# Products with the values: two quads of heads one behind the other, and scores by single heads

## What is computed

```python
q, k, v = _split_heads(query, W_Q), _split_heads(key, W_K), _split_heads(value, W_V)
scores = jnp.einsum('bhqd,bhkd->bhqk', q, k) / np.sqrt(D_K)
scores = jnp.where(mask[:, None, :, :] == 1, -1e9, scores)
p = jax.nn.softmax(scores, axis=-1)
ctx = jnp.einsum('bhqk,bhkd->bhqd', p, v)
out = jnp.einsum('bsd,ed->bse', concat(ctx), W_O) + residual
mu, var = mean(out), mean((out - mu) ** 2)
return (out - mu) * rsqrt(var + LN_EPS) * gamma + beta
```

## Time and profile before

| | us |
|---|---|
| median of 3 runs | 192.54 (192.52 to 193.17) |
| the profiled execution | 192.26 |
| its span, first to last instruction | 190.4 |
| TensorE busy | 160.2 (84%) |
| VectorE busy | 138.4 (73%) |
| GpSimd busy | 104.9 (55%) |
| ScalarE busy | 100.7 (53%) |
| block 0 (starts at 28.02) | 26.0 |
| block 1 (starts at 54.02) | 20.1 |
| blocks 2, 3 and 4 | 18.3 each |
| blocks 5 and 6 | 15.3 and 13.7 |

### The profile page before, as it was taken

How to read it: one execution, slowest core, us unless ns; L and a number is a source line. 1 busy time by engine, 2 the same in 40 slices (tenths; PEclk the granted TensorE clock), 3 DMA queues, 4 the chain that set the end, 5 groups by cost and what they waited for, 6 DMA issues and landing times.

```text
span 190.4 us, 3486 instructions
## 1 busy us (share of the span) xinstructions
PE 160.2 (84%) x1208; PEld 86.2 (45%) x1208; DVE 138.4 (73%) x300; ACT 100.7 (53%) x133; POOL 104.9 (55%) x128
## 2 busy tenths in 40 slices
PE   7697939798869999999999999999899898977300
PEld 7454515343324466445544554564455363534200
DVE  1775533875856669788978897798989965685993
ACT  3242144634544664666755875587577679473400
POOL 6002441434544371349597959664744946858990
PEclk9999996999988999999999999999999999999955
DMA  5959988746989985873596664747350051020115
GB/s 174 358 152 159 284 210 237 220 121 114 275 218 229 232 205 149 246 233 102 161 280 176 186 195 131 204 129 218 135 201 0 3 179 46 6 104 0 54 56 220
DMA packets 23083, 31.42 MB, mean 165 GB/s; under 512 B 3459, under 2 KB 18611, under 8 KB 23067
## 3 DMA queue, kind: packets, MB, share of 16 engines
q1 hardware_dynamic: 22234, 29.98, 55.4%
q10 hardware_dynamic: 832, 1.23, 2.0%
HBM read 11.28 MB, written 4.19 MB: 81 GB/s over the span
## 4 chain that ended last, share of the span: by engine, by line
PE 61%; DVE 13%; DMA 12%; ACT 4%; issue 4%; POOL 2%; SPq 1%; DVEq 1%; POOLq 0%; ACTq 0%
PE pv_ps L818 14%; PE work_ps L828 13%; PE work_ps L761 11%; PE scores_ps L809 11%; PE max_ps L782 8%; DVE neg_max L599 4%; DMA R<-neg_max_t 4%; DMA x_t<-in_x_cols 3%; DMA R<-first_max_t 3%; DMA R<-q 2%; DVE ctx_q L607 2%; ACT probs L496 2%; POOL y L366 1%; ACT not_full L450 1%; DVE var_eps_last L723 1%
## 5 line engine op out<-in xcount | busy, mean ns | idle before, releaser
L496 ACT ACTIVATE probs<-scores_ps 77x1024 f32<-77x1024 f32 x64 | 64.6, 1017 | 47.6 <-PE scores_ps L809 42.3
L599 DVE TENSOR_REDUCE neg_max<-max_ps 128x6 f16<-128x462 f32 (+1 forms) x84 | 45.6, 566 | 13.9 <-PE max_ps L782 13.8
L809 PE MATMUL scores_ps<-R,kb 126*77 126x512 f16 x128 | 39.7, 394 | 3.7 <-DMA R<-first_max_t 1.9
L782 PEld LDWEIGHTS max_ps<-kb,R 125*128 125x128 f16 x512 | 27.1, 100 | 34.3 <-DVE neg_max L599 16.9
L339 POOL TENSOR_TENSOR q<-q 128x512 f16<-128x512 f32 x14 | 16.2, 1155 | 43.6 <-ACT q L457 43.6
L818 PE MATMUL pv_ps<-probs,v_all 77*32 77x512 f32 x256 | 34.3, 608 | 4.2 <-ACT probs L496 3.5
L782 PE MATMUL max_ps<-kb,R 125*128 125x77 f16 x512 | 32.8, 202 | 3.4 <-DVE neg_max L599 2.5
L346 POOL TENSOR_TENSOR ctx_n<-ctx_q,rden 128x256 f32<-128x256 f32 x32 | 20.1, 628 | 21.9 <-DVE rden L609 21.8
L607 DVE STREAM_TRANSPOSE ctx_q<-pv_ps 128x512 f32<-128x512 f32 x32 | 22.8, 711 | 10.1 <-PE pv_ps L818 9.7
L828 PE MATMUL work_ps<-wo_t,ctx_e 128*128 128x256 f32 x112 | 26.9, 382 | 0.0
L761 PE MATMUL work_ps<-x_t,wq_t 128*128 128x512 f32 x48 | 24.6, 635 | 0.4
(11 more groups left out here) (70 smaller groups left out, 143.6 us busy)
## 6 DMA issues: line engine op xcount, KB each, us to landing
R<-mask_t SPq DMA_DIRECT2D x14, 616.0 KB
R<-q SPq DMA_DIRECT2D x48, 128.0 KB
x_t<-in_x_cols SPq DMA_DIRECT2D x8, 512.0 KB, 6.7
y<-in_x SPq DMA_DIRECT2D x8, 512.0 KB, 4.7
out<-y SPq DMA_DIRECT2D x7, 512.0 KB, 2.6
mask_i<-in_mask_cols SPq DMA_DIRECT2D x8, 154.0 KB
out<-y SPq DMA_DIRECT2D x2, 256.0 KB, 2.9
kb<-k SPq DMA_DIRECT2D x12, 38.5 KB, 3.3
```

Of the source, the lines that this page charges most:

```text
L496: nc.scalar.activation(probs[:, s, :, :], scores_ps[s % 2][0:KEYS, :, :], ACT.Exp).then_inc(exp_done, 1)
L599: nc.vector.tensor_reduce(to[:, t, lo:hi], max_ps[u % 2][:, 0:(hi - lo) * KEYS].rearrange("p (h k) -> p h k", k=KEYS), AX.X, ALU.max, nega ...
L782: last = nc.tensor.matmul(max_ps[u % 2][:, (h - lo) * KEYS:(h - lo + 1) * KEYS], R[m % R_RING][0:MAX_ROW, h, t * P:(t + 1) * P], kb[0:MAX_ ...
L809: last = nc.tensor.matmul(scores_ps[s % 2][0:KEYS, i, :], kb[:, 2 * s + i, n // PER_BATCH, :], R[n % R_RING][:, 2 * s + i, :], start=True, ...
```

## The change

The eight banks are dealt out anew: three banks for scores, each of one head, two for the maximum units as before, two for quads (`pv_both`) and one for the rest. Each head's scores now have their own semaphore step, and the product of a head waits for the exponential of the head three before. ScalarE's exponential is one instruction for each head, 77x512.

The quads move. Step 4 of block n does quads 0 and 1, and step 0 of block n + 1 quads 2 and 3. In the last block quad 2 stands in step 6, and quad 3 after the last step, as before. VectorE's turns follow in the same steps, its turning back of the second half goes from step 1 to step 2, and GpSimd's divisions move accordingly. The wait for the scaled queries of block 1 stands ahead of block 0 and not in it, since their projection now uses a bank of scores and one of quads.

The diff, cut to its core:

```diff
@@ -60,6 +60,11 @@
 Y_RING = 4
 R_RING = 3
 
+SCORES_RING = 3
+MAX_RING = 2
+
+PV_RING = 2
+
 
 def loaded_R(m):
 
...
@@ -155,9 +160,10 @@
         rstd_last = sb("rstd_last", [P, TILES])
         warm_sb = sb("warm_sb", [P, 2])
 
-        scores_ps = [ps(f"scores_ps{i}", [P, 2, BLOCK]) for i in range(2)]
-        max_ps = [ps(f"max_ps{i}", [P, BLOCK]) for i in range(2)]
-        pv_ps = ps("pv_ps", [P, BLOCK])
+        scores_ps = [ps(f"scores_ps{i}", [P, BLOCK]) for i in range(SCORES_RING)]
+        max_ps = [ps(f"max_ps{i}", [P, BLOCK]) for i in range(MAX_RING)]
+        pv_both = [ps(f"pv_ps{i}", [P, BLOCK]) for i in range(PV_RING)]
+        pv_ps = pv_both[0]
         work_ps = ps("work_ps", [P, BLOCK])
         max16 = max_ps[0][:, :].bitcast(F16)
         pv16 = pv_ps[:, :].bitcast(F16)
...
@@ -165,8 +171,8 @@
         k_ps = [max_ps[0][:, 0:PAIR_KEYS], max_ps[1][:, 0:PAIR_KEYS],
                 work_ps[:, 0:PAIR_KEYS], work_ps[:, PAIR_KEYS:2 * PAIR_KEYS]]
         k_second = work_ps[:, 0:2 * PAIR_KEYS].rearrange("p (e c) -> p e c", e=HALVES)
-        q_ps = [[scores_ps[m][:, e, :] for e in range(HALVES)] for m in (0, 1)]
-        last_ps = [max_ps[0][:, 0:D], max_ps[1][:, 0:D], scores_ps[0][:, 0, 0:D], scores_ps[0][:, 1, 0:D]]
+        q_ps = [[scores_ps[0][:, :], scores_ps[1][:, :]], [scores_ps[2][:, :], pv_both[1][:, :]]]
+        last_ps = [max_ps[0][:, 0:D], max_ps[1][:, 0:D], scores_ps[0][:, 0:D], scores_ps[1][:, 0:D]]
 
         s_wq, s_wk, s_wv, s_wo, s_ctx, s_gb = (sem(f"s_{c}") for c in ("wq", "wk", "wv", "wo", "ctx", "gb"))
         s_xt = [sem(f"s_xt{i}") for i in range(X_RING)]
...
@@ -393,16 +399,16 @@
             mask_product(2)
             eq(3)
             q_lo(2, 0)
-            norm(0, 0)
             q_lo(2, 1)
+            norm(0, 0)
             norm(0, 1)
             mask_product(3)
             q_lo(3, 0)
-            norm(0, 2)
             eq(4)
             q_lo(3, 1)
 
             for n in range(1, N):
+                norm(n - 1, 2)
                 norm(n - 1, 3)
                 if n >= 3:
                     times_gamma(n - 3, 1)
...
@@ -422,9 +428,9 @@
                 norm(n, 1)
                 if n + 4 < N:
                     eq(n + 4)
-                norm(n, 2)
                 if n >= 2:
                     times_gamma(n - 2, 0)
+            norm(N - 1, 2)
             times_gamma(N - 3, 1)
             norm(N - 1, 3)
             moments(N - 2)
...
@@ -486,14 +492,16 @@
                 nc.scalar.activation(neg_max_t[:, :], max16[0:HEADS, 0:BLOCK], ACT.Copy).then_inc(nm_ready, 1)
                 act.wait_ge(nm_ready, m)
                 if m >= R_RING:
-                    act.wait_ge(scores_done, PAIRS * (m - R_RING + 1))
+                    act.wait_ge(scores_done, HEADS * (m - R_RING + 1))
                 act.dma_start(R[m % R_RING][MAX_ROW:ROWS, :, :], neg_max_t[:, :]).then_inc(s_nm, 16)
 
             def exp(n, s):
-                act.wait_ge(scores_done, PAIRS * n + s + 1)
                 if n > 0:
                     act.wait_ge(pv_done, QUADS * (n - 1) + s // 2 + 1)
-                nc.scalar.activation(probs[:, s, :, :], scores_ps[s % 2][0:KEYS, :, :], ACT.Exp).then_inc(exp_done, 1)
+                for i in range(2):
+                    head = HEADS * n + 2 * s + i
+                    act.wait_ge(scores_done, head + 1)
+                    nc.scalar.activation(probs[:, s, i, :], scores_ps[head % SCORES_RING][0:KEYS, :], ACT.Exp).then_inc(exp_done, 1)
 
             def apply(m, t):
                 if t == 0:
...
@@ -691,10 +699,14 @@
                     for m, u in before:
                         reduce_max(m, u)
                     if s == 0 and n >= 1:
+                        turn(n - 1, 2)
                         turn(n - 1, 3)
-                    if s in (2, 4, 6):
-                        turn(n, s // 2 - 1)
-                    if s == 1 and n >= 1:
+                    if s == 4:
+                        turn(n, 0)
+                        turn(n, 1)
+                    if s == 6 and last:
+                        turn(n, 2)
+                    if s == 2 and n >= 1:
                         turn_back(n - 1, 1)
                     if s in (3, 5) and n >= 2:
                         stats(n - 2, (s - 3) // 2)
...
@@ -803,19 +815,19 @@
                             pe.wait_ge(s_first[g], 16)
                 elif s == 0:
                     pe.wait_ge(s_nm, 16 * n)
-                if PAIRS * n + s >= 2:
-                    pe.wait_ge(exp_done, PAIRS * n + s - 1)
                 for i in range(2):
-                    last = nc.tensor.matmul(scores_ps[s % 2][0:KEYS, i, :], kb[:, 2 * s + i, n // PER_BATCH, :],
-                                            R[n % R_RING][:, 2 * s + i, :], start=True, stop=True)
-                last.then_inc(scores_done, 1)
+                    head = HEADS * n + 2 * s + i
+                    if head >= SCORES_RING:
+                        pe.wait_ge(exp_done, head + 1 - SCORES_RING)
+                    nc.tensor.matmul(scores_ps[head % SCORES_RING][0:KEYS, :], kb[:, 2 * s + i, n // PER_BATCH, :],
+                                     R[n % R_RING][:, 2 * s + i, :], start=True, stop=True).then_inc(scores_done, 1)
 
             def values(n, t):
-                pe.wait_ge(exp_done, PAIRS * n + 2 * (t + 1))
-                if QUADS * n + t >= 1:
-                    pe.wait_ge(pv_turned, QUADS * n + t)
+                pe.wait_ge(exp_done, HEADS * n + 4 * (t + 1))
+                if QUADS * n + t >= PV_RING:
+                    pe.wait_ge(pv_turned, QUADS * n + t + 1 - PV_RING)
                 for j in range(4):
-                    last = nc.tensor.matmul(pv_ps[32 * j:32 * (j + 1), :], v_all[:, n // PER_BATCH, 4 * t + j, :],
+                    last = nc.tensor.matmul(pv_both[t % PV_RING][32 * j:32 * (j + 1), :], v_all[:, n // PER_BATCH, 4 * t + j, :],
                                             probs[:, 2 * t + j // 2, j % 2, :], start=True, stop=True)
                 last.then_inc(pv_done, 1)
 
...
@@ -871,15 +883,13 @@
             count(2)
             pe.wait_ge(first_ready, 1)
             turn_first_max(1)
-            pe.wait_ge(q_scaled, HALVES)
+            pe.wait_ge(q_scaled, 2 * HALVES)
             pe.wait_ge(tail_ones, 16)
 
             for n in range(N):
                 last_block = n == N - 1
                 for s in range(STEPS):
                     before, behind = split_units(n, s)
-                    if n == 0 and s == 1:
-                        pe.wait_ge(q_scaled, 2 * HALVES)
                     scores(n, s)
                     for m, u in before:
                         max_unit(m, u)
...
@@ -901,9 +911,13 @@
                             pe.wait_ge(q_scaled, 3 * HALVES + 1)
                             project_q(3, 1, work_ps[:, :])
                     if s == 0 and n >= 1:
+                        values(n - 1, 2)
                         values(n - 1, 3)
-                    if s in (2, 4, 6):
-                        values(n, s // 2 - 1)
+                    if s == 4:
+                        values(n, 0)
+                        values(n, 1)
+                    if s == 6 and last_block:
+                        values(n, 2)
                     if n == 0 and s == 4:
                         pe.wait_ge(q_scaled, 3 * HALVES)
                         count(3)
```

16 lines of the change are left out of this document (8 added, 8 removed).

## The result

The changed kernel takes 199.62 us, the median of four runs (198.13 to 202.72), against 192.53 before (four runs, 191.66 to 193.17). The ratio is 1.035, 95% interval 1.029 to 1.041: slower. Ratios compare fast runs alone, those less than 1.5% above the fastest run of their kernel, and none is given where only one run of a kernel is fast. The forecast was 198.1 us, with a range of 194.3 to 201.0. The profiled execution took 198.13 us with a span of 196.1.

A forecast was written before the change was run, and what follows sets the result against it. TensorE paces the middle blocks, with VectorE 3 us a block behind. -0.1 + 1.3 + 2.9 + 0.4 - 0.05 + 1.2 = +5.6 us on 192.26 gives 197.9, median 198.1 us; range 194.3 to 201.0.

The forecast's parts named there:

- The join: Second of two adjacent quads, in steps 4 and 0: 0.21 us saved a join, bounds 0 and 0.24, 15 joins.
- Steps 2 and 3: Middle blocks: first maximum unit of step 3 waits for VectorE until 7.47; block 0.36 us late instead of 0.21 early.
- Steps 5 to 7: Middle blocks: 6a, 6b, 7a (step 6's two maximum units, step 7's first) wait for VectorE; saves 0.27, not 1.09 us.
- Blocks 5 and 6: +0.4 us in block 5, which has no query half; -0.05 us in block 6, whose late steps have no units.
- Block 0 and the start: Block 0 gains about 0.1 us, as its landing DMA sets the end; change predicted for its start 0.
- Block 1: A middle block plus 0.3 us for a quad more at 1.2 GHz; +1.2 us with block 0's 0.1.
- Block 7 and the tail: +1.2 us: GpSimd's shift, awaited by ScalarE before the last exponentials, comes 1.2 later; the end behind is the same work.
- ScalarE and GpSimd: 128 exponentials of 0.60 us, 12 us more busy, cost nothing elsewhere; GpSimd's second division ends at 17.6, hidden by 0.4.
- the faster one: Rival: VectorE has 2.9 us of slack a block, so no new waits at the maximum units; 190.3 us, chance 0.10.
- the half one: Rival: waits of steps 5 to 7 met, those of steps 2 and 3 and the tail not; about 195.4 us, chance 0.16.
- the one of the join: Rival: two quads in a row save nothing, 15 x 0.21 us more; 201.3 us, chance 0.06.
- the starving ring: Rival: ScalarE's ring of three starves TensorE, two gaps of 0.43 us in five blocks; about 200.3 us, chance 0.07.

The follow-up runs named there:

- the two experiments with the product of zeros: Eight-column product of zeros added to the changed kernel: between the two quads of a pair 202.38 us, ahead of the first quad 196.36 us.
- the clock kept up: Empty products of zeros in TensorE's three long waits: changed kernel 194.88 us, ratio 1.014; kernel with new banks and old quad places 190.18 us, ratio 0.987.

## Why the prediction was right

**The join**: 0.88 for the first of two quads and nothing ahead of the second. Measured were 1.85 a pair and 0.24 saved. The rule of the Trainium skill that was set against it (TensorE: Matmul & The Clock Gate, Part 3), as the prediction reads it, would have made the two experiments with the product of zeros equal; they differ by 0.49 a middle block. The traces here don't bear that reading out for these tiles. The same section also lets weights load ahead into the background weight buffer, a clause that the prediction left out; no run here tells the two ways apart.

**Steps 2 and 3**: the second query half was to start at 7.62 after the block's start, and started at 7.60 (119.93 less 112.33). The pair of step 4 alone gives +0.33 for a predicted +0.36.

**Step 4**: step 5's units were to come at 14.21, and came at 14.17.

**Steps 5 to 7**: predicted 15.32, 15.86, 17.02 and 19.25 for 6a, 6b, 7a and the next block. The rows say 15.28, 15.82, 17.05 and 19.28. The pair of step 0 alone gives +0.66 for a predicted 0.88 - 0.27 = 0.61. (The walk's own times, 14.21 and 19.25, give 0.29 saved and not 0.27, and +0.95 a block.) These terms, three middle blocks, carry 2.9 of the 5.6.

**Blocks 5 and 6**: +0.34 and -0.07 for +0.37 and -0.05. With the clock kept up they are +0.44 and +0.02.

**Block 0 and the start**: the landing DMA sets the end, as said. Block 0 started 0.9 late in the profiled execution, waiting for the load of the first maxima, and took 0.85 less where 0.1 was predicted; block 1 began at 54.07 and 54.02. TensorE's part of it is 0.16, as large as forecast. The other 0.7 is the transfer (6.0 us instead of 6.7), which the prediction took as fixed. That it made up for the late start is chance.

**Block 1** was wrong as the profile shows it, +1.27 predicted and -0.36 seen, and right in its larger part. 0.97 of it was the middle block's and the hidden quad's; with the clock kept up the same difference is +1.04, and taking the hidden quad back gave 0.85. The other 0.3, more work at 1.2 GHz, assumed that the slow stretch is there in each execution. It was in the profiled one of before and not in that of after, and so the difference of the two profiles took about 1.4 us off this term (1.04 and 0.36).

**Block 7 and the tail** were sized too small, 1.2 for 2.77. The mechanism is the one named: ScalarE's row waits for GpSimd's shift, and the last exponentials stand behind it. The row in after, beside the earlier trace rows:

```profile
174.70 1.09 ACT L509 ACTIVATE y<-y,shift,rstd 128x256 f32<-128x256 f32 x2 [0.52 <-POOL shift L365]
```

From the block's start that is 13.78, and it was 12.00: +1.78 where the prediction had 1.2. Step 5 came at 9.52 instead of 7.97, 1.55 later; the prediction had 1.1 (9.1 and 8.0). GpSimd's row of it begins 11.81 after the block's start and was at 10.02. VectorE's last statistics before it end 1.55 later too (11.48 and 9.93). Another 0.24 is GpSimd's own: it waits 2.98 us for the first turn of step 4, and the division of that quad and a row of beta, which were long done before, now stand just ahead of the shift:

```profile
170.80 0.62 POOL L352 TENSOR_TENSOR ctx_n<-ctx_q,rden 128x256 f32<-128x256 f32 x1 [2.98 <-DVE rden L617]
171.37 1.27 POOL L378 TENSOR_TENSOR y<-y,beta_sb 128x512 f32<-128x512 f32 x1
172.73 0.23 POOL L360 TENSOR_SCALAR var_eps<-mean_var 128x4 f32<-128x4 f32 x1
```

The remaining 0.93 is the clock: "The end behind it is the same work" held for the work, but it ran at 1.2 GHz. With empty products in the wait it went away. It doesn't hang on the moved quads alone: the last quad took 1.94 after a wait of 1.79 with single quads at the ends, and 1.06 after 1.79 with the banks alone and after 2.04 with the product ahead of the pairs. Single quads in block 7 didn't shorten the tail, so that how to place them there stays open.

**ScalarE and GpSimd**: 587 ns for a predicted 600, and 3.3 us more busy in all. "12 us more busy" in the prediction was worked out from 0.60 x 128 against 64.6; the records of two in a row overlap, and a busy time counts an overlap once. A head waits for an exponential in blocks 6 and 7, as predicted, but in blocks 0 and 5 as well (0.68 and 0.34 us by the rows of block 0, 0.16 in block 5); in the middle blocks none does. GpSimd's second division ends 17.69 after the start (predicted 17.6), still in time.

**The sum**: +5.6 predicted, +5.87 between the profiled executions (198.13 and 192.26). Two errors of 1.6 us, in block 1 and in the tail, cancel; that is luck. With the clock kept up in both, the moved quads cost 5.4 us of span. There the middle blocks are right again, and two other errors cancel for the most part: block 0 and its start, -0.85 for -0.1 (0.2 of it by the empty products), and block 7, +1.80 for +1.2.

The medians differ by 7.1, and here the account is less complete. By the ratios, the banks alone gave 1.3% (0.987, interval 0.977 to 0.997), which the prediction had at nothing. The moved quads cost 2.7% with the clock kept up (1.014 over 0.987), about 5.2 us. Without the empty products the changed kernel is another 2.1% slower (1.035 over 1.014), about 4 us, and the kernel with the banks alone isn't slower (0.987 both times). The intervals of these ratios reach 0.5 to 1.0% to each side, so that these sizes are rough; as far as they go, the changed kernel lost more to the clock, and the prediction had 0.3 us for that. How that is spread over the runs isn't shown, since only the profiled executions have a trace. The changed kernel's mean clock was 0.949 to 0.950 in three further runs and 0.958 in the profiled one, which was 1.2 to 1.6 us faster than they. The range held because the gain of the banks, the loss to the clock and the errors at both ends of the kernel partly made up for each other; the walk of the middle blocks needed no such luck.

Of the rivals, the faster one and the half one are out by the waits at 3a, 6b and 7a, the one of the join by the two products of zeros, and the starving ring by the kernel with the banks alone, whose middle blocks are 18.28. Two of the prediction's side sums are a little off: its half case comes to 195.2 and not 195.4, and the rival in which the join saves nothing, 201.3, lies just outside the range that is said to hold both slower rivals.

## What to carry to other kernels

A short piece of work that stands between two uses of a ring of two buffers is the time in which the other engine empties them. Moving it next to work of its own kind saves a switch (0.24 us a pair here), but the waits that it had covered come into the open: with the switch already saved, each moved pair cost 0.33 or 0.66 us a block. Walk both engines' queues from the rows' distances before moving it; with this, the starts in a middle block came out within 0.05 us. And compare profiles of two kernels only with the granted clock of each stretch beside them, because a stretch at 1.2 GHz in one of them is as large as what is looked for.
